# A relational graph layer on one core: messages for unsorted edges, carried in the sorted rows, and added as 16-bit parts

## The chip, the cores and the metric

One core of one Trainium2 chip. The metric is the device time of one execution in microseconds. TensorE is called PE here, VectorE DVE, ScalarE ACT, GpSimd POOL and SyncE SP, as the profile has them.

## What is computed

A stack of four graph layers over 3125 nodes of 32 features and 53125 edges, each behind a layer norm with relu and with a residual. The change touches the first, a relational layer used twice in a row:

```python
def _rel_layer(x, src, dst, etypes, V, a, w_loop, bias, activation=None):
    W = jnp.einsum('rb,bio->rio', a, V)              # 20 relations from 8 bases, 32x32 each
    seg = dst.astype(jnp.int32) * R + etypes.astype(jnp.int32)
    agg = jax.ops.segment_sum(x[src], seg, num_segments=N * R)
    agg = agg.reshape(N, R, -1)
    h = jnp.einsum('nri,rio->no', agg, W) + x @ w_loop + bias
    if activation is not None:
        h = activation(h)
    return h
h = _rel_layer(x, src, dst, etypes, V1, a1, w_loop1, bias1, activation=relu)
h = _rel_layer(h, src, dst, etypes, V2, a2, w_loop2, bias2)
```

That is: each edge carries `x[src] @ W[type]` to its destination node, where the messages are added up. All of it is float32.

## The kernel before

Nodes lie in 25 blocks of 128 (`NB`), one node to a partition. Edges are dealt with in tiles of 128; there are 440 tiles (`T`) once the edges are sorted by the block of their destination and each block is padded to whole tiles. Edges as they come fill 416 columns of 128 (`EC`).

`sort_edges` has two stages. In the first, DVE makes masks of the destination blocks (25 of 128x416), a running count over all of them (one scan of 10400 elements), and, with three small products of PE, the row in the sorted order of every edge (`row`). POOL makes constants and zeroes the records. In the second stage POOL issues one indirect DMA for each of the 416 columns, which scatters the edges' records of 20 words (edge attributes, a one, destination in block, source, type) into `sorted_edges` in DRAM. Beside this, DVE makes the relation weights of both layers from the bases (`relation_weights`, 15 operations each) and the layer norm, PE turns the nodes and makes the message table (`table_stage`: for every node and relation the message of 32 words, 50 products of 320 columns, written to `message_table` in DRAM by SP), and `block_limits` prepares arrays for the last layer.

`add_up_pass` then adds the messages of a layer, in 40 groups of 11 sorted tiles. Of each group 8 tiles have their messages gathered from `message_table` by POOL, an indirect DMA each; for the other 3 they are made on the spot: DVE makes one-hots of the source nodes (25 of 128x384, `sources`), PE picks the nodes' three 16-bit parts with them (`pick`, 25 products), multiplies by the basis parts (`basis_products`) and makes the type's coefficients (`coefficients`), DVE weighs and sums (`weigh`, `messages`). Every tile is added into the accumulator in PSUM by a float32 product of its destination one-hot (made by DVE, `onehots`) with the messages, at a column offset that PE reads from a table (`add`). In the first layer this pass begins with reading the sorted records back, making indices from them (`edge_indices`), and turning source and type rows for the broadcasts of SP (`edge_rows`).

After the first layer the table stage runs again for the second (`after_first`), then `add_up_pass` for it, then three other layers. The order on each engine is the order of the program; the engines wait for one another by semaphores, and the functions in a `with nc.Block()` form a stage, at whose end all engines meet. The steps to follow are `sort_edges` (from line 196, scatters at line 393), `edge_indices` (line 475), `table_stage` (line 624), `add_up_pass` (gathers at 732, source one-hots at 795, terms at 812, sums at 821, picks at 870, adding at 861), `after_first` (line 959).

## Time and profile before

| | |
|---|---|
| time, median of 3 runs | 3484.52 us (3481.57 to 3484.59) |
| profiled execution, its own time | 3477.77 us |
| its span, first to last instruction | 3476.0 us |
| PE busy | 2507.7 us (72%) |
| DVE busy | 2620.6 us (75%) |
| ACT busy | 547.8 us (16%) |
| POOL busy | 2312.8 us (67%) |
| mean granted clock of PE | 0.809 |

A share of busy time is a mean over stages that are bound by different engines, so the profile is read stage by stage: a view by stretches of time first, then the groups of equal instructions, and the timeline where stages meet. POOL's busy time in a transfer is that of making it; the transfer lands later. The granted clock of PE is a share of 2.4 GHz; it takes two levels, 1.2 and 2.4 GHz.

### The profile page before, as it was taken

Reading aid. Unit: us, or ns where it says so; the run is one execution under the profiler, and the core shown is the slowest. Engines: PE = TensorE matmul, PEld = TensorE weight load, DVE = VectorE, ACT = ScalarE, POOL = GpSimd, SP = SyncE. Lnnn points to the kernel's source line nnn. Section 1 sums busy time; section 2 is a strip of 40 time slices with the busy share of each in tenths; the row PEclk is TensorE's granted clock in tenths of the full one; section 3 lists DMA queues with packets and bytes.
Section 4 is the critical chain, followed back from the end, with each engine's and each line's share of the span. In section 5 each row is a group of like instructions: output and inputs, shape, how many; then the busy total and the mean of one; then the engine's idle time right before and its main releaser. Section 6 shows DMA issues by size and latency. Waiting matters only on the chain. (4 is left out here: it accounts for less than half of the span.)

```text
span 3476.0 us, 55173 instructions
## 1 busy us (share of the span) xinstructions
PE 2507.7 (72%) x18522; PEld 1736.9 (50%) x18632; DVE 2620.6 (75%) x7995; ACT 547.8 (16%) x1243; POOL 2312.8 (67%) x2253
## 2 busy tenths in 40 slices
PE   0600000699998999987999699999999867777752
PEld 0300000577875777764666466666666533333331
DVE  9400000799993999979999788888888479999987
ACT  0100000000001000000111122222222123333320
POOL 2777777677770777757777477777777177777740
PEclk9655555688885888878999799999999878888885
DMA  6300000211113111111111100000001011111120
GB/s 100 107 8 8 8 8 8 81 24 26 24 18 100 29 26 25 24 13 34 29 28 28 14 12 11 11 11 11 11 11 11 1 32 27 27 27 27 27 17 5
DMA packets 125181, 91.52 MB, mean 26 GB/s; under 512 B 59702, under 2 KB 110838, under 8 KB 124278
## 3 DMA queue, kind: packets, MB, share of 16 engines
q0 software_dynamic: 70912, 41.10, 8.8%
q1 hardware_dynamic: 54006, 46.92, 5.7%
q8 instruction: 164, 2.69, 0.3%
q14 instruction: 99, 0.81, 0.1%
HBM read 60.45 MB, written 27.41 MB: 25 GB/s over the span
## 5 line engine op out<-in xcount | busy, mean ns | idle before, releaser
L732 POOL DMA_INDIRECT rel_rows<-message_table,message_indices x640 | 645.0, 1008 | 280.1 <-issue 194.5
L1287 POOL DMA_INDIRECT flow_x<-node_table,src_indices x440 | 539.4, 1226 | 227.1 <-issue 104.8
L795 DVE TENSOR_SCALAR rel_source_onehot<-rel_sources,node_numbers 128x384 bf16<-128x384 f16 x2000 | 535.1, 306 | 6.1 <-PE p_rel_picked L870 5.7
L393 POOL DMA_INDIRECT sorted_edges<-stage,sorted_row x416 | 404.3, 972 | 192.0 <-issue 126.5
L1657 POOL DMA_INDIRECT att_kv_rows<-kv_table,att_index x440 | 423.9, 963 | 141.2 <-issue 129.2
L1429 PE MATMUL flow_acc_bwd<-flow_onehot_j,flow_by_q 128*128 128x270 bf16 (+1 forms) x2530 | 493.4, 325 | 7.1 <-issue 0.2
L870 PE MATMUL p_rel_picked<-rel_source_onehot,rel_h_parts 128*96 128x384 bf16 x2000 | 428.5, 383 | 1.0 <-issue 0.7
L870 PEld LDWEIGHTS p_rel_picked<-rel_source_onehot,rel_h_parts 128*96 128x96 bf16 x2000 | 293.6, 148 | 124.6 <-issue 3.8
L1038 POOL DMA_INDIRECT sum_rows<-node_table,src_indices x280 | 270.4, 966 | 110.7 <-issue 85.0
L761 DVE COPY p_rel_lanes<-iota 128x128 f32<-128x128 f32 x2 | 0.6, 295 | 439.4 <-PEq L388 436.7
L664 PE MATMUL p_rel_terms<-ident,source_centred 128*128 128x128 f32 (+1 forms) x4 | 1.1, 435 | 455.2 <-DVE source_centred L650 455.2
L1693 DVE TENSOR_REDUCE att_tile_max<-p_att_scores 128x4 f32<-128x512 f32 x440 | 283.7, 684 | 25.8 <-PE p_att_scores L1807 21.4
L1073 DVE TENSOR_SCALAR sum_source_onehot<-sum_sources,node_numbers 128x512 bf16<-128x512 f16 x1000 | 300.6, 367 | 0.0
L1126 PE MATMUL p_sum_picked<-sum_source_onehot,sum_h_stack 128*96 128x512 bf16 x1000 | 248.8, 411 | 36.8 <-DVE sum_source_onehot L1073 36.3
L1805 PE MATMUL p_att_scores<-att_mask,identb 128*128 128x512 bf16 x440 | 198.2, 450 | 67.0 <-ACT att_parts_turned L1741 67.0
L782 DVE TENSOR_TENSOR rel_onehot<-p_rel_lanes,dst_in_block 128x128 f32<-128x128 f32 x880 | 239.8, 273 | 0.0
L1426 PE MATMUL flow_acc_fwd<-flow_messages,flow_onehot 128*128 128x32 bf16 x1320 | 235.4, 178 | 0.0
L664 PEld LDWEIGHTS p_rel_terms<-ident,source_centred 128*128 128x128 f32 (+1 forms) x4 | 0.7, 202 | 456.5 <-DVE source_centred L650 456.5
L844 ACT CAST rel_picked<-p_rel_picked 96x384 bf16<-96x384 f32 x80 | 38.0, 474 | 1102.1 <-PE p_rel_picked L870 1102.1
L1341 DVE TENSOR_TENSOR flow_by_q<-flow_messages,source_q_mask 128x512 bf16<-128x512 bf16 x330 | 207.2, 681 | 0.0
L1807 PE MATMUL p_att_scores<-att_parts_turned,att_pick 96*128 96x512 bf16 x440 | 201.9, 459 | 0.0
L1426 PEld LDWEIGHTS flow_acc_fwd<-flow_messages,flow_onehot 128*128 128x128 bf16 x1320 | 129.0, 98 | 145.5 <-issue 26.6
(281 smaller groups left out, 4647.5 us busy)
## 6 DMA issues: line engine op xcount, KB each, us to landing
message_table<-message_rows SPq DMA_DIRECT2D x50, 320.0 KB, 2.1
rel_rows<-message_table,message_indices POOLq DMA_INDIRECT x640, 2.5
rel_sources<-source_rows SPq DMA_DIRECT2D x80, 96.0 KB
flow_x<-node_table,src_indices POOLq DMA_INDIRECT x440
att_kv_rows<-kv_table,att_index POOLq DMA_INDIRECT x440, 2.4
sorted_edges<-stage,sorted_row POOLq DMA_INDIRECT x416, 2.1
sum_sources<-source_rows SPq DMA_DIRECT2D x40, 128.0 KB, 3.1
sum_rows<-node_table,src_indices POOLq DMA_INDIRECT x280, 2.4
```

Source lines behind the costliest of these rows:

```text
L393: pool.indirect_dma_start(out=d["sorted"], out_offset=bass.IndirectOffsetOnAxis(ap=row[:, c:c + 1], axis=0), in_=stage[:, c, :], in_offset ...
L732: pool.indirect_dma_start(out=rows[b][:, t, :], out_offset=None, in_=d["messages"], in_offset=bass.IndirectOffsetOnAxis(ap=s["idx_msg"][:, ...
L795: last = dve.tensor_scalar(which[g % 2][:, c, :], srcs[b][:], s["node"][:, c:c + 1], None, ALU.is_equal)
L870: last = pe.matmul(pp[g % 2][0:3 * F, 0:RW], hs[:, c].rearrange("p k f -> p (k f)"), which[g % 2][:, c, :], start=(c == 0), stop=(c == NB ...
L1038: pool.indirect_dma_start(out=rows[b][:, t, :], out_offset=None, in_=d["nodes"], in_offset=bass.IndirectOffsetOnAxis(ap=s["idx_src"][:, g ...
L1073: last = dve.tensor_scalar(which[g % 2][:, c, :], srcs[g % bufs][:], node[:, c:c + 1], None, ALU.is_equal)
L1126: last = pe.matmul(pp[g % 2][0:3 * F, 0:PT * P], hs[:, c].rearrange("p k f -> p (k f)"), which[g % 2][:, c, :], start=(c == 0), stop=(c == ...
L1287: pool.indirect_dma_start(out=X[b][:, t, 0:F], out_offset=None, in_=d["nodes"], in_offset=bass.IndirectOffsetOnAxis(ap=s["idx_src"][:, g * ...
L1426: pe.matmul(accF[:, bass.ds(cols[b, t], F)], hot[b][:, t, :], top(M[b][:])[:, k, t, 0:F], start=False, stop=True, skip_group_check=True)
L1429: last = pe.matmul(accB[:, lo:hi], S[b][:, t, k, :], J[b][:, t, lo:hi], start=False, stop=True, skip_group_check=True)
L1657: pool.indirect_dma_start(out=KV[b][:, t, :], out_offset=None, in_=d["kv"], in_offset=bass.IndirectOffsetOnAxis(ap=ibuf[b][:, t:t + 1], ax ...
L1693: dve.tensor_reduce(tm[b][:, 0, t, :], pR[t % PR][:].rearrange("p (h e) -> p h e", h=HEADS), AX_X, ALU.max).then_inc(max_ready, 1)
```

## The change

Sorting and the making of messages become one stage. The messages of the first layer are made for the edges as they come, in 69 groups of six columns (`CG`): for four (`CP`) by one-hot products as in `add_up_pass`, now 512 wide, for two by gathers from the message table; a tail of two columns is gathered. The messages are put into slots of a ring behind the edge's record, so that a row has 52 words (`ROW`) instead of 20, and POOL scatters each column's rows to their places in the sorted order. DVE has the layer norm ahead of the scan; the relation weights are made by PE from turned bases and coefficients, 32 products a layer; ACT copies the message table out of PSUM and issues its writes; the counts, the limits' turn and the tile map are put between the table products of PE. Rows of padding are written by one DMA from a small tile.

A new stage, `add_sorted`, reads the sorted rows in 20 loads of 22 tiles. ACT and DVE split the messages into three 16-bit parts, DVE makes the destination one-hots of a load in one 16-bit operation, and PE adds with one product of 96 columns for each tile, the three parts side by side; DVE adds the three in the end. The turned rows, the indices for the second layer and the block limits are made at the end of this stage. The second layer's `add_up_pass` is as it was. The semaphores are cleared once more, between the two stages.

The core of the diff (declarations, loads and the unchanged rank steps left out):

```diff
+ROW = REC + F
+CG, CP, SLOTS, RINGS = 6, 4, 6, 4
+AHEAD, BESIDE = 4, 11
...
+                sort_edges(nc, a, s, d, sb, ps, sem, W2)
+                clear_semaphores()
+                relational_layers(nc, a, s, d, sb, ps, sem, W2)
...
+            def _(pool):
...
-                    pool.memset(s["rec"][:], 0.0).then_inc(recs, 1)
...
+                def scatter(g):
+                    b = g % SLOTS
+                    js, c0 = columns(g)
+                    pool.wait_ge(filled, g + 1)
+                    if g < CN:
+                        pool.wait_ge(msg_ready, g + 1)
+                    pool.wait_ge(gathered[b], 16 * (CG - CP) * (g // SLOTS + 1))
+                    for j in js:
+                        c = c0 + j - js[0]
+                        pool.indirect_dma_start(
+                            out=d["sorted"], out_offset=bass.IndirectOffsetOnAxis(ap=row[:, c:c + 1], axis=0),
+                            in_=ring[b][:, j, :], in_offset=None).then_inc(sent[b], 16)
+
+                for g in range(AHEAD):
+                    gather(g)
+                pool.wait_ge(row_ready, 1)
+                pool.wait_ge(pads, 16)
+                for g in range(CN + 1):
+                    if g + AHEAD <= CN:
+                        gather(g + AHEAD)
+                    scatter(g)
...
+            def _(act):
...
+                def fill(g):
+                    slot_free(act, g)
+                    js, c0 = columns(g)
+                    lo, n = js[0], len(js)
+                    act.copy(ring[g % SLOTS][:, lo:lo + n, 0:FE], attr[:, c0:c0 + n, :])
+                    act.copy(ring[g % SLOTS][:, lo:lo + n, FE:REC], meta[:, c0:c0 + n, :]).then_inc(filled, 1)
...
+            def _(dve):
...
+                def sources(g):
+                    b = g % RINGS
+                    dve.wait_ge(row_in[b], 32 * (g // RINGS) + 32)
+                    if g >= 2:
+                        dve.wait_ge(pick_done, g - 1)
+                    for c in range(NB):
+                        last = dve.tensor_scalar(which[g % 2][:, c, :], srcs[b][:], s["node"][:, c:c + 1], None,
+                                                 ALU.is_equal)
+                    last.then_inc(which_ready, 1)
...
+                for g in range(CN):
+                    sources(g)
+                    if g >= 2:
+                        weigh(g - 2)
+                    types(g)
+                    if g >= 2:
+                        messages(g - 2)
...
+            def _(pe):
...
+                def weights(i, banks):
+                    pe.wait_ge(w_in, 64)
+                    v3 = basis[i].rearrange("b (i o) -> b i o", o=F)
+                    for o in range(F):
+                        j, at = divmod(o, F // 2)
+                        last = pe.matmul(banks[j][0:F, at * R:(at + 1) * R], v3[:, :, o], coefT[i][:],
+                                         start=True, stop=True)
+                    last.then_inc(w_made, 1)
...
+                    if n == 2 * BESIDE:
+                        counts()
+                    elif n == 2 * BESIDE + 4:
+                        limits_turned()
+                    elif n == 2 * BESIDE + 6:
+                        tile_map()
...
+                for g in range(CN):
+                    pick(g)
+                    if g >= 1:
+                        basis_products(g - 1)
+                    coefficients(g)
+                basis_products(CN - 1)
...
+LT, LBUFS, HBUFS = 22, 4, 3
+LOADS = T // LT
+PARTED = 3 * F
+def add_sorted(nc, a, s, d, sb, ps, sem, init, finish):
...
+                    for c in range(LOADS):
+                        b = c % LBUFS
+                        act.wait_ge(rows_in[b], 16 * (c // LBUFS) + 16)
+                        if c >= HBUFS:
+                            act.wait_ge(used, c - HBUFS + 1)
+                        act.copy(msg[c % HBUFS][:, :, 0, :], rows[b][:, :, REC:ROW]).then_inc(first_ready, 1)
+                        if c >= 1:
+                            second_part(c - 1)
+                        act.copy(s["dstl"][:, c * LT:(c + 1) * LT], rows[b][:, :, DSTL])
+                        act.copy(s["rec"][:, c * LT:(c + 1) * LT, :], rows[b][:, :, 0:REC]).then_inc(rec_taken, 1)
...
+                        dve.tensor_tensor(hot[c % HBUFS][:], s["iotab"][:].unsqueeze(1).to_broadcast([P, LT, P]),
+                                          dstb[:, mine].unsqueeze(2).to_broadcast([P, LT, P]), ALU.is_equal)\
+                            .then_inc(hot_ready, 1)
+                        if c >= 1:
+                            third_part(c - 1)
+                        dve.wait_ge(first_ready, c + 1)
+                        if c >= 2:
+                            dve.wait_ge(third_ready, c - 1)
+                        dve.tensor_tensor(left[c % 2][:], rows[b][:, :, REC:ROW], msg[c % HBUFS][:, :, 0, :],
+                                          ALU.subtract).then_inc(rest_ready, 1)
...
+                        pe.wait_ge(hot_ready, c + 1)
+                        pe.wait_ge(third_ready, c + 1)
+                        for t in range(LT):
+                            col = pe.snap(regs[t // RG][t % RG], min_val=0, max_val=NB // 5 * BANK - PARTED - F)
+                            last = pe.matmul(acc[:, bass.ds(col, PARTED)], hot[c % HBUFS][:, t, :],
+                                             msg[c % HBUFS][:, t].rearrange("p k f -> p (k f)"),
+                                             start=False, stop=True, skip_group_check=True)
+                        last.then_inc(used, 1)
...
-def relation_weights(a, s, sb, sem, st, layer):
...
-def edge_indices(s, d, sb, sem, st):
```

## Rows read from the trace of the kernel before

In the view by stretches (rows 1) a row has the stretch in us, its length, and for PE, the weight loads PEld, DVE, ACT and POOL the busy time and the count of instructions; then the granted clock, the DMA engines' busy share and GB/s. A timeline row has the start in us, the duration, the engine (an ending q is its queue), the line and operation with the tiles written and read, a count where rows are merged, and the idle time before it with what ended it. A group's row has the line, engine, operation, tiles and shapes, the count, the busy time and the mean in ns, and the idle time ahead.

**Rows 1.** Busy time of each engine by stretch: length, engines, granted clock, DMA.

```profile
77.00:617.00 540.00, 60.98 (x131) 36.23 (x131) 53.66 (x81) 11.70 (x27) 404.35 (x417) 0.53 0.10 24
617.00:652.00 35.00, 13.27 (x60) 12.59 (x61) 22.14 (x69) 0.00 (x0) 22.14 (x25) 0.50 0.52 168
652.00:1061.00 409.00, 397.98 (x2480) 320.17 (x2478) 397.28 (x1522) 26.11 (x80) 301.29 (x298) 0.83 0.16 23
1061.00:1112.00 51.00, 48.91 (x111) 29.55 (x112) 15.61 (x29) 8.93 (x21) 0.00 (x0) 0.53 0.34 129
1600.00:1900.00 300.00, 275.92 (x1833) 180.91 (x1834) 300.00 (x980) 31.65 (x66) 228.01 (x237) 0.93 0.16 29
```

**Rows 2.** Timeline, end of the scatters: start us, us, engine, line.

```profile
607.24 0.96 POOL L393 DMA_INDIRECT sorted_edges<-stage,sorted_row  x1 [0.30 <-issue]
...
616.99 0.16 POOL L721 IOTA node_numbers<- 128x25 f32 x1 [8.78 <-POOLq L388]
...
622.46 0.27 DVE L475 TENSOR_SCALAR index_scratch<-records 128x110 f32<-128x110 f32 x1 [5.16 <-DMA records<-sorted_edges]
```

**Rows 3.** Costliest groups: line, operation, count, busy us, mean ns.

```profile
L732 POOL DMA_INDIRECT rel_rows<-message_table,message_indices x640 | 645.0, 1008 | 280.1 <-issue 194.5
...
L1038 POOL DMA_INDIRECT sum_rows<-node_table,src_indices x280 | 270.4, 966 | 110.7 <-issue 85.0
...
L1341 DVE TENSOR_TENSOR flow_by_q<-flow_messages,source_q_mask 128x512 bf16<-128x512 bf16 x330 | 207.2, 681 | 0.0
```

**Rows 4.** Timeline of the sum layer, one-hots and picks.

```profile
1706.39 3.04 DVE L1073 TENSOR_SCALAR sum_source_onehot<-sum_sources,node_numbers 128x512 bf16<-128x512 f16 x10
...
1708.27 5.57 PE L1126 MATMUL p_sum_picked<-sum_source_onehot,sum_h_stack 128*96 128x512 bf16 x25
...
1716.88 7.28 PE L1126 MATMUL p_sum_picked<-sum_source_onehot,sum_h_stack 128*96 128x512 bf16 x25 [1.00 <-DVE sum_source_onehot L1073]
```

**Rows 5.** Timeline of the second layer's pass, DVE, terms and their sums.

```profile
1235.99 0.94 DVE L812 TENSOR_TENSOR rel_terms<-p_rel_terms,rel_coef 128x768 f32<-128x768 f32 x1
...
1237.18 0.93 DVE L821 TENSOR_REDUCE rel_messages<-rel_terms 128x96 f32<-128x768 f32 x1
```

**Rows 6.** Timeline of the second layer's pass, PE, small products of one group.

```profile
1390.18 0.83 PE L887 MATMUL p_rel_coef<-rel_type_coef,rel_type_onehot 20*128 20x8 f32 x6
...
1391.63 1.19 PE L897 MATMUL p_rel_terms<-rel_basis_parts,rel_picked 96*128 96x256 bf16 x9
```

**Rows 7.** Timeline, a scatter beside DVE's relation weights.

```profile
83.64 1.39 POOL L393 DMA_INDIRECT sorted_edges<-stage,sorted_row  x1 [0.30 <-issue]
...
84.23 0.81 DVE L556 TENSOR_TENSOR w_rel_term<-coef,basis 32x640 f32<-32x640 f32 x1
```

**Rows 8.** Timeline of the opening, POOL and DVE.

```profile
3.30 7.43 POOL L287 MEMSET records<- 128x8800 f32 x1
...
3.41 7.55 DVE L305 TENSOR_SCALAR block_ends<-dst_in 128x416 int32<-128x416 int32 x1 [2.43 <-DMA dst_in<-in_dst]
...
19.44 21.82 DVE L312 TENSOR_TENSOR_SCAN rank<-block_mask 128x10400 f32<-128x10400 f32 x1
...
46.46 14.13 DVE L340 SCALAR_TENSOR_TENSOR rank<-rank,block_offset,block_mask 128x416 f32<-128x416 f32 x25
...
74.43 0.16 DVE L358 TENSOR_TENSOR sorted_row<-sorted_row,extra_row 128x1 uint32<-128x1 uint32 x1
```

**Rows 9.** Timeline, where the first layer's sums are taken.

```profile
1061.32 0.99 DVE L959 TENSOR_SCALAR h_nodes<-rel_acc 128x800 f32<-128x800 f32 x1 [5.47 <-PEq L717]
```

**Rows 10.** Timeline, PE, node turns and the message table.

```profile
100.74 5.71 PE L519 MATMUL p_turn<-ident,h_nodes 128*32 128x128 f32 x25 [52.53 <-DVEq L595]
...
107.10 51.57 PE L624 MATMUL p_message<-w_rel,h_transposed 32*128 32x320 f32 x100 [0.66 <-DVE h_transposed L528]
```

**Rows 11.** Timeline, DVE, first and last step of the block limits.

```profile
171.92 0.38 DVE L430 CAST tile_blocks<-dst_columns 1x440 f32<-1x440 int32 x1
...
180.08 0.18 DVE L439 COPY any_tile_rows<-p_limits 128x25 f32<-128x25 f32 x1
```

813 lines of the change are left out of this document (520 added, 293 removed).

## The prediction

> **What bounds the kernel now.** I read the busy times by stage first, then the costliest groups, then the timeline at the seams of the stages. By stage [rows 1], the first relational layer takes 1061 of the 3476 us of the span, in four pieces: 77 us in which rows of the sorted order are worked out, 540 us of scatters, 35 us of reading back, and 409 us of adding up. In the 540 us POOL is busy for 404 us and everything else for less than 61: the 416 scatters bind alone. In the 409 us PE (398) and DVE (397) are both full and POOL has 301. A POOL transfer costs 1.26 us from start to start: 0.96 us and 0.30 us before the next one [rows 2]. The 320 gathers of this layer's pass are half of the 640 of [rows 3], at 1.008 + 0.30 us. So POOL waits for PE and DVE in one stage, and they wait for POOL in the other. The change puts the two kinds of work side by side. What it costs is a longer start, ahead of that common stage, and a separate stage for adding.
>
> **The common stage, one group.** It has 69 groups of six columns (4 picked by one-hot products, 2 gathered) and a tail of two gathered columns.
> DVE: 25 source one-hots 128x512. Ten in a row took 3.04 us [rows 4], so 25 x 0.30 = 7.5. The terms and the sums are 1024 wide instead of 768: 0.94 and 0.93 us [rows 5] times 4/3, less the 0.07 by which one overlaps the next, 1.15 each. Type one-hot: the two start 1.19 us apart with it between them [rows 5], so 1.19 - 0.87 = 0.32, and 0.4 at 512 columns. Sum 10.2 us.
> POOL: 8 transfers. With the idle DVE's 0.96 it is 8 x 1.26 = 10.1 us; with the 1.008 of the pass with mixed one-hots [rows 3] 8 x 1.31 = 10.5; with the 0.966 beside 512-wide one-hots [rows 3] 10.1. Rows of 208 B instead of 80 B are not shown, but 128 B gathers at 0.966 and 80 B scatters at 0.96 differ by nothing. I take 10.1 to 10.2, nearest to the 512-wide row.
> PE: pick 5.57 us at full clock and 7.28 where the clock fell within it [rows 4]; 12 basis products 4/3 of 1.19 = 1.6; four coefficient products 4/3 of 0.83 = 1.1 [rows 6]. That is 8.3 to 10.0. The sum layer, with the same pick of 25 x 512, was granted 0.93 on average [rows 1].
> ACT fills the slots (two more copies in a group), far below 10 us. SP's two broadcasts per group run three groups ahead.
> All three come out near 10.2, and DVE, POOL and PE hand on to one another; for that I add 0.05: **10.25 us a group**, with ends 10.1 (POOL's cheapest, the one-hots a little closer) and 10.8 (POOL at 1.31, and a little of PE's waits).
>
> **A rule against it.** Beside DVE work a POOL transfer can be longer: with two-input f32 products on DVE a scatter took 1.39 us, not 0.96 [rows 7]. The Trainium skill, SBUF — State Buffer, "SBUF: two separate sides", says that GpSimd cannot write DMA descriptors while DVE holds their shared port pair in a two-port mode; by that, scatters moved under DVE's one-hots would be starved. The trace agrees for the memset and DVE's shift that ran together, 7.43 and 7.55 us [rows 8], and does not for the one-hots: 0.966 us beside them [rows 3]. The terms read PSUM and one SBUF operand, the sums one, so no two-input products stand in the new loop. What a starved POOL would give is the second rival.
>
> **The start, on the path.** Before, DVE's chain ran from the scan (19.4 us) to row numbers at 74.6 us [rows 8]. Now the layer norm lies ahead of the scan: five 128x800 steps of 1 us and small ones [rows 9], 6 us; and the 7.43 us zeroing of the records, beside which DVE's shift waited, is gone; I put the scan at 21 us and its end at 43. Then the counts need PE, which has them in its queue behind the relation weights, the turns and 23 table products. Relation weights: 64 products with 20 columns; the nearest row, the coefficient products, gives 0.25 each [rows 6], the bounds are 0.13 and 0.25, I take 0.2: 13 us. They start when edge columns have been turned, about 12 us: 25 us. The turns take 5.7, the table 51.57 / 50 = 1.03 us a product at half clock [rows 10]: 31 + 23.7 = 55 us. So DVE waits about 12 us for PE (0 if PE keeps its full clock; 16 with the dearer weights). Making the weights on PE frees DVE, which was idle beside the scatters before: worth nothing there, and on the path here. Four more table products, then the limits, 61 us; DVE's 28 us of ranks [rows 8], 89; indices, and the splits of h and of the basis (six steps of 1 us, small ones), 98. The table has been written by about 88 (31 + 52 + the waits for DVE and the landing), so the first 8 gathers (10 us) hide under that. The pad rows, 11.7 MB now, have from 10 to 98 us. Three rounds of one-hots (7.5 each) and the first terms: the first messages are ready at **125 us** (bounds 112 and 135). Before, POOL began at 77: this start costs 48 us.
>
> **The end of it.** 125 + 68 x 10.25 + the last group's six and the tail's two scatters at 1.26 = 832 us. From the last scatter to the next stage 8.8 us passed before [rows 2]; the added clearing of semaphores is bounded by 0 and that, I take 3: **844 us**.
>
> **Adding up sorted rows.** 20 loads of 586 KB; the earlier 1.1 MB reads had the first at DVE after 5.5 us [rows 2], I take 4.5. Per load DVE makes one 128x2816 one-hot from two 16-bit operands, one of them broadcast along its inner axis: the nearest row, a 16-bit product with such an operand, took 0.681 us for 512 [rows 3], about one element a cycle, so 2816 x 1.04 ns + 0.07 = 3.0; at the one-hots' 0.30 for 512 it would be 1.65. Two subtractions of 704 elements at 0.99 for 800 [rows 9] make 1.75 less overlaps, 1.6; the small copy and waits 0.3: **4.9 us, 98 in all** (bounds 70 and 105). PE has 22 products of 96 columns in that time, well below 4.9 us, and ACT four copies of some 2.2 us together. Then 5 reductions of 480 (3 us), last parts and products (4), relu (1), turned edge rows and indices (5; done inside the 35 us stage before), and the block limits, 8.4 us [rows 11], which lay beside scatters before and now have nothing to hide them: 21. Sum 4.5 + 98 + 21 = 124 us, so 968 us. Before, the same point, h ready for the second table, was at 1062 us [rows 9]. **Gain 94 us.** The gathers go from 320 to 140, which is 235 us of POOL; the start takes back 48, the adding 124, less 35 us of reading back, and the adding products leave PE's full pass.
>
> The rest of the kernel issues the same work. The profiled execution took 3477.8 us, 1.8 around its span; the median of the runs is 6.7 above it. 3477.8 - 94 = 3384 for a profiled one; against the median **3390 us**.
>
> **Rivals.** First, PE binds. If the clock stayed at its lower level in the new loop (1.2 GHz), pick and basis products would take twice 5.57 and 1.6, with 1.1 15.4 us a group: + 5.15 x 69 = 355, 3745 us, slower than before. It decides from a chain above 10.25 us, and above 11.6 nothing of the gain is left. For it: 1.1 us of tiny products and 2 us of idleness each group, and 0.53 granted through the second table stage, where PE was busy for 49 of 51 us [rows 1]. Against: 0.93 in the sum layer with the same pick, where 3 us of small products follow it. Chance 0.05.
> Second, POOL is starved: at 1.39 + 0.30 a group is 13.5 us, + 225, 3615 us; it needs 0.17 us more per transfer to eat the gain. Chance 0.06.
> Third, the stages do side by side what they did, and the gain is lost in hand-overs: 11.6 us a group, about 3484, no change that shows. Chance 0.03.
> Fourth, as forecast but with the large one-hot at two elements a cycle (- 27) and PE at full clock in the table (- 12): 3351. Chance 0.10.
>
> **How the numbers follow.** The forecast holds 0.76; its range is 3365 (125 - 13, 10.1) to 3440 (10.8 a group is + 38, start + 10). With the fourth rival, 3345 to 3450. A measurement of this kernel tells about 0.2% (7 us) from no change. Faster: 0.76 + 0.10, and 0.02 of the second rival, where the transfers grow by less than 0.17 us: 0.88; same 0.03; slower 0.05 + 0.04 = 0.09.
>
> **What would show it.** Right: POOL starts its scatters at about 125 us and is busy to about 832 with 0.95 to 1.0 us each; DVE is 98% busy there; the group repeats every 10.1 to 10.5 us; the adding stage's DVE one-hot of 3.0 us repeats every 4.9; the second layer's turns start near 968. Wrong: PE's granted clock near 0.5 in the loop and DVE waiting for the terms; scatters above 1.15 us; a first scatter after 150 us; a wait for the pad rows; or PE, not DVE, setting the 4.9 us.

## Result and the profile after

The changed kernel took 3405.14 us, median of 4 runs (3402.48 to 3406.53), beside 3484.56 us for the kernel before (4 runs on the same chip): a ratio of 0.9772, 95% interval 0.9758 to 0.9786, which is 79 us less (75 to 84). The forecast was 3390 us, a gain of 94. So the direction and the mechanism came out; 15 us of the gain did not. The profiled execution of after took 3402.48 us, its span is 3400.5, and PE's mean granted clock is 0.845 (before 0.809).

Busy time by stretch, the view of [rows 1], for the changed kernel: length, then PE, PE's weight loads, DVE, ACT and POOL, then granted clock, share of the DMA engines, GB/s.

```profile
0.00:117.00 117.00, 71.14 (x269) 43.94 (x269) 74.03 (x109) 32.64 (x75) 12.41 (x28) 0.62 0.76 217
117.00:144.00 27.00, 19.01 (x90) 11.40 (x91) 25.08 (x84) 2.10 (x8) 4.68 (x5) 0.77 0.08 18
144.00:852.00 708.00, 589.04 (x3019) 364.24 (x3018) 678.12 (x1857) 70.44 (x270) 532.86 (x546) 0.89 0.15 33
852.00:866.00 14.00, 12.76 (x57) 11.22 (x56) 11.06 (x9) 5.58 (x11) 0.00 (x0) 0.50 0.70 226
866.00:968.00 102.00, 56.44 (x430) 44.20 (x428) 84.89 (x72) 35.67 (x69) 0.00 (x0) 0.50 0.29 85
968.00:992.00 24.00, 12.04 (x51) 6.64 (x50) 15.56 (x33) 0.00 (x0) 0.00 (x0) 0.55 0.04 9
```

What were two stages, 540 us in which POOL worked alone and 409 us in which PE and DVE were full [rows 1], is one stage of 708 us in which DVE is busy 96% of the time, POOL has 546 transfers, and PE's clock is 0.89. Ahead of it stand 144 us instead of 77, behind it an adding stage in which PE's granted clock is 0.50. No run lays the two kinds of work one behind the other again: that the gain comes from putting them side by side is read from these stretches of before and after. The costliest groups of that stage, from the page (line, operation, count, busy us, mean ns, idle time before them and what ended it):

```profile
L594 DVE TENSOR_SCALAR block_table<-in_sources,node_numbers 128x512 bf16<-128x512 f16 x1725 | 520.0, 371 | 0.8 <-PE p_in_picked L706 0.6
...
L414 POOL DMA_INDIRECT sorted_edges<-block_table,sorted_row x416 | 406.3, 977 | 147.8 <-issue 147.8
...
L400 POOL DMA_INDIRECT block_table<-message_table,message_index_in x140 | 136.5, 975 | 144.6 <-DMA message_table<-message_rows 102.2
```

One group of DVE in the timeline (start us, us, operation); the next group's one-hots start 10.18 us after these:

```profile
508.49 7.59 DVE L594 TENSOR_SCALAR block_table<-in_sources,node_numbers 128x512 bf16<-128x512 f16 x25
516.01 1.20 DVE L609 TENSOR_TENSOR block_table<-p_in_terms,block_table 128x1024 f32<-128x1024 f32 x1
517.14 0.47 DVE L601 TENSOR_SCALAR block_table<-in_types,lane_number 20x512 f32<-20x512 f16 x1
517.54 1.20 DVE L617 TENSOR_REDUCE block_table<-block_table 128x128 f32<-128x1024 f32 x1
518.67 3.50 DVE L594 TENSOR_SCALAR block_table<-in_sources,node_numbers 128x512 bf16<-128x512 f16 x11
```

The start, in the timeline of SP's queue, DVE and POOL, then the lines of ACT and DVE from the view of waits up to 110 us (us in total, times, longest) and two lines of the page's list of DMA issues (KB each, us from issue to landing):

```profile
8.98 0.63 SPq L331 DMA_DIRECT2D sorted_edges<-pad_rows  x1
9.66 42.11 SPq L334 DMA_DIRECT2D records<-in_edge_attr  x1
...
75.34 0.18 DVE L529 TENSOR_SCALAR total_counts<-p_in_picked 128x25 f32<-128x25 f32 x1 [34.05 <-PE p_in_picked L661]
...
117.23 7.61 DVE L594 TENSOR_SCALAR block_table<-in_sources,node_numbers 128x512 bf16<-128x512 f16 x25
...
143.28 6.63 DVE L594 TENSOR_SCALAR block_table<-in_sources,node_numbers 128x512 bf16<-128x512 f16 x25
...
144.14 5.89 POOL L414 DMA_INDIRECT sorted_edges<-block_table,sorted_row  x1 [21.24 <-issue]
150.34 0.97 POOL L414 DMA_INDIRECT sorted_edges<-block_table,sorted_row  x1 [0.30 <-issue]
...
842.20 0.96 POOL L414 DMA_INDIRECT sorted_edges<-block_table,sorted_row  x1 [0.30 <-issue]
```

```profile
ACT message_rows L466 <- DMA message_table<-message_rows: 42.6, 12, 14.7
DVE total_counts L529 <- PE p_in_picked L661: 34.0, 1, 34.0
...
sorted_edges<-pad_rows SPq DMA_DIRECT2D x1, 11440.0 KB, 54.7
...
message_table<-message_rows ACTq DMA_DIRECT2D x25, 320.0 KB, 2.2
```

DVE waits 34 us for the block counts. PE makes them after 23 of the 50 table products, and these stand still because ACT, which empties their banks, waits 42.6 us until the table's blocks have been written. Meanwhile the padding, issued at 8.98 us, is under way for 54.7 us: the table's writes issued up to 55 us land after 6.8 to 16.5 us, most of the later ones after 2.2. (The edge attributes, 3320 KB on the same queue, are read in that time too; no run takes them out, so their share of the waits is open.) From the counts on everything comes in the forecast's spacing.

In the adding stage a load's products, DVE's one-hot with its wait, and DVE's sums at the end:

```profile
908.05 2.94 PE L887 MATMUL rel_acc<-rel_message_parts,rel_onehot 128*128 128x96 bf16 x22 [2.88 <-issue]
913.07 2.87 PE L887 MATMUL rel_acc<-rel_message_parts,rel_onehot 128*128 128x96 bf16 x22 [2.08 <-issue]
...
911.10 3.09 DVE L844 TENSOR_TENSOR rel_onehot<-iota_bf,rel_dst_bf 128x2816 bf16<-128x2816 bf16 x1 [1.04 <-PE rel_acc L887]
...
969.54 2.92 DVE L858 TENSOR_REDUCE h_nodes<-rel_acc 128x160 f32<-128x480 f32 x5 [9.24 <-PE rel_acc L887]
```

PE is idle for 2.1 to 2.9 us ahead of 22 products that take 2.9, waiting for nothing that the profile shows; at this place the program reads the column numbers into registers. DVE, whose own work for a load repeats every 4.83 us where it is not held (863.89 to 868.72 in the timeline), waits for PE.

### The profile page after: what moved, and what is told of

It is laid out like the page before. It is cut to its first block and busy times, and to the rows that moved or that the text cites. A ratio compares the mean times of both kernels' runs of the same rounds, so it can differ in the third digit from the quotient of the medians.

```text
span 3400.5 us, 58425 instructions
## 1 busy us (share of the span) xinstructions
PE 2791.8 (82%) x19728; PEld 1844.5 (54%) x19838; DVE 2957.7 (87%) x8386; ACT 653.1 (19%) x1566; POOL 2125.8 (63%) x2076
## 5 line engine op out<-in xcount | busy, mean ns | idle before, releaser
L706 PE MATMUL p_in_picked<-block_table 128*96 128x512 bf16 x1725 | 446.1, 422 | 106.4 <-DVE block_table L594 106.4
L594 DVE TENSOR_SCALAR block_table<-in_sources,node_numbers 128x512 bf16<-128x512 f16 x1725 | 520.0, 371 | 0.8 <-PE p_in_picked L706 0.6
L1086 POOL DMA_INDIRECT rel_rows<-message_table,message_indices x320 | 322.7, 1008 | 300.2 <-POOLq L1303 203.0
L414 POOL DMA_INDIRECT sorted_edges<-block_table,sorted_row x416 | 406.3, 977 | 147.8 <-issue 147.8
L706 PEld LDWEIGHTS p_in_picked<-block_table 128*96 128x96 bf16 x1725 | 229.5, 136 | 297.2 <-DVE block_table L594 93.6
L1139 DVE TENSOR_SCALAR rel_source_onehot<-rel_sources,node_numbers 128x384 bf16<-128x384 f16 x1000 | 266.6, 306 | 7.0 <-PE p_rel_picked L1212 6.8
L400 POOL DMA_INDIRECT block_table<-message_table,message_index_in x140 | 136.5, 975 | 144.6 <-DMA message_table<-message_rows 102.2
L1212 PE MATMUL p_rel_picked<-rel_source_onehot,rel_h_parts 128*96 128x384 bf16 x1000 | 217.8, 387 | 0.2 <-issue 0.2
L1467 PEld LDWEIGHTS p_sum_picked<-sum_source_onehot,sum_h_stack 128*96 128x96 bf16 x1000 | 130.2, 133 | 141.6 <-DVE sum_source_onehot L1414 37.9
L1770 PEld LDWEIGHTS flow_acc_bwd<-flow_onehot_j,flow_by_q 128*128 128x128 bf16 x2640 | 161.9, 96 | 56.8 <-issue 36.1
## 6 DMA issues: line engine op xcount, KB each, us to landing
sorted_edges<-pad_rows SPq DMA_DIRECT2D x1, 11440.0 KB, 54.7
```

Source lines behind the costliest of these rows:

```text
L414: pool.indirect_dma_start(out=d["sorted"], out_offset=bass.IndirectOffsetOnAxis(ap=row[:, c:c + 1], axis=0), in_=ring[b][:, j, :], in_offs ...
L594: last = dve.tensor_scalar(which[g % 2][:, c, :], srcs[b][:], s["node"][:, c:c + 1], None, ALU.is_equal)
L706: last = pe.matmul(pp[g % 2][0:3 * F, 0:CW], hs[:, c].rearrange("p k f -> p (k f)"), which[g % 2][:, c, :], start=(c == 0), stop=(c == NB ...
L1086: pool.indirect_dma_start(out=rows[b][:, t, :], out_offset=None, in_=d["messages"], in_offset=bass.IndirectOffsetOnAxis(ap=s["idx_msg"][:, ...
L1467: last = pe.matmul(pp[g % 2][0:3 * F, 0:PT * P], hs[:, c].rearrange("p k f -> p (k f)"), which[g % 2][:, c, :], start=(c == 0), stop=(c == ...
L1770: last = pe.matmul(accB[:, lo:hi], S[b][:, t, k, :], J[b][:, t, lo:hi], start=False, stop=True, skip_group_check=True)
```

## Experiments

Theory: the change gains as forecast, by putting POOL's transfers beside DVE's and PE's picks; the missing 15 us lie in the start, where the padding holds the table and the table holds the counts, and in the adding stage, where PE's register loads bind and not DVE. The rivals for each are in the expectations. All ratios are against the kernel before, run beside them; the changed kernel stands at 0.9772, and 0.001 is 3.5 us. From the sums of the adding stage to the end all these kernels issue the same work, and that remainder took 2430 to 2442 us in their profiles, in no relation to the edit. So a whole time tells a stage's gain to some 6 us either way, and the timeline tells it better. "First scatter" is its start, "sums" the start of DVE's sums at the end of the adding stage, both in the profiled run.

| run | ratio to before | first scatter, us | last scatter's end | sums |
|---|---|---|---|---|
| changed kernel | 0.9772 (0.9758 to 0.9786) | 144.1 | 843.2 | 969.5 |
| e1 wide padding | 0.9754 (0.9735 to 0.9774) | 133.4 | 834.1 | 960.6 |
| e2 counts first | 0.9737 (0.9721 to 0.9753) | 126.8 | 825.9 | 952.3 |
| e8 both | 0.9705 (0.9684 to 0.9726) | 114.6 | 814.8 | 941.0 |
| e5 one register load | 0.9745 (0.9728 to 0.9763) | 145.7 | 845.8 | 960.1 |
| e6 third part on POOL | 0.9775 (0.9757 to 0.9793) | 146.4 | 845.7 | 970.1 |
| e7 first scatter free | 0.9789 (0.9770 to 0.9808) | 143.2 | 844.9 | 971.7 |
| e9 start and registers | 0.9664 (0.9642 to 0.9686) | 115.6 | 815.2 | 929.6 |
| e10 four table buffers | 0.9662 (0.9644 to 0.9680) | 110.9 | 810.0 | 924.5 |
| e11 f32 adding | 1.0044 (1.0025 to 1.0062) | 146.9 | 846.0 | 1056.6 |

### The start: padding and counts

```diff
-PADS = 5
+PADS = 20
```

> The padding rows are written in pieces of 4160 B instead of 1040 B (20 rows in a piece instead of 5); nothing else changes. In the changed kernel that write lands 54.7 us after its issue, ACT waits 42.6 us for the message table's own writes meanwhile, and the block counts are done at 74.9 us. Theory (the padding write holds the DMA engines against the table): if its time goes by the piece it lands in 14 to 35 us, the counts are done at 50 to 60 us, the first scatter starts at 122 to 132 instead of 144.1, and the whole takes 3384 to 3393 us. Rival 1 (its time goes by the byte): it still lands after about 50 us or more, counts at about 75, no change in the time (3402 to 3408). Rival 2 (the table is slow for another reason: PE at half clock, two output buffers): it lands sooner, but the counts stay later than 65 us and the time falls by less than 8 us.

The padding took 35.3 us instead of 54.7, so its time goes with the piece as well as with the byte. DVE had the counts at 64.97 us, the first scatter came 10.8 us earlier, the sums 9.0. So the padding does hold the start; but the theory's 50 to 60 us for the counts was missed, since ACT still waited 29.9 us for the table's writes. The whole time fell by 6 us, less than the stage, and its interval overlaps that of the changed kernel. By these numbers rival 2 (the two output buffers) is as near as the theory, and the run with four table buffers, below, shows that it has its part.

```diff
-AHEAD, BESIDE = 4, 11
+AHEAD, BESIDE = 4, 4
...
-                    elif n == 2 * BESIDE + 4:
+                    elif n == 2 * BESIDE + 1:
                         limits_turned()
-                    elif n == 2 * BESIDE + 6:
+                    elif n == 2 * BESIDE + 2:
                         tile_map()
```

> PE makes the block counts after 8 of the 50 table products instead of after 22, and the two small products that follow them one product later each instead of four and six later. Theory (DVE's 34 us wait for the counts is the lost part of the start): the counts are done at 42 to 46 us, row numbers at 76 to 80 instead of 108.8, the first source one-hots at 84 to 88 instead of 117.2. The first pick then waits for PE's table (107), so the first scatter comes at 122 to 128 instead of 144.1, and the whole takes 3383 to 3390 us. Rival (the table's writes hold everything, not the counts): PE, held for DVE inside the table, ends it 5 us or more later, gathers and picks start after 112, and the time falls by less than 10 us.

```profile
43.66 0.19 DVE L529 TENSOR_SCALAR total_counts<-p_in_picked 128x25 f32<-128x25 f32 x1 [1.14 <-PE p_in_picked L661]
...
126.84 5.90 POOL L414 DMA_INDIRECT sorted_edges<-block_table,sorted_row  x1 [5.84 <-issue]
```

DVE's wait of 34.05 us became 1.14, and the first scatter came 17.3 us earlier, as forecast, and not by the whole 34: now DVE's third run of one-hots waits 18.6 us for the first pick, which stands behind the table on PE. The table itself lost nothing (the first gather at 108.7 us instead of 110.3). The 17 us arrive at the sums undiminished.

> The padding in pieces of 4160 B and the counts after 8 table products together. e1 brought the first scatter from 144.1 to 133.4 us (gathers could begin at 99.8 instead of 110.3), e2 to 126.8 (gathers at 108.7, first scatter 18.2 us behind them). Theory (two separate holds on the start: the counts for DVE's chain, the table's writes for PE's first pick): gathers begin at 96 to 101, the first scatter starts at 114 to 120, 24 to 30 us earlier than in the changed kernel, and the stage behind it ends as much earlier: 3374 to 3383 us. Rival (they are one and the same hold): the first scatter stays at 124 to 128 and the time at that of e2, about 3392.

First scatter at 114.6, 29.6 us earlier; the sums 28.5 earlier. That is the sum of e1 and e2 (10.8 + 17.3) within 2 us: two holds, one on DVE's chain and one on the table, and not one and the same.

### The common stage: who binds it

In this run the gathers are left out, and the scatters of the gathered columns read the slots of picked ones:

```diff
                 def gather(g):
-                    b = g % SLOTS
-                    slot_free(pool, g)
...
+                    pass
...
-                            in_=ring[b][:, j, :], in_offset=None).then_inc(sent[b], 16)
+                            in_=ring[b][:, j % CP, :], in_offset=None).then_inc(sent[b], 16)
```

> The 140 gathers are left out; the columns that were gathered are scattered with the messages of picked columns in their place. POOL has 6 transfers a group instead of 8, 7.6 us instead of 10.16; DVE, PE and ACT have the work of before. Theory (DVE binds the common stage, POOL only just fits): the group repeats every 10.0 to 10.2 us, DVE over 97% busy, the time falls by 0 to 15 us. Rival 1 (POOL binds, DVE would be faster if let): the group falls below 9.7 us, the time by more than 35 us. Rival 2 (DVE's one-hots are slowed by POOL's descriptors): 25 one-hots take clearly less than 7.59 us.

```diff
-                    for c in range(NB):
+                    for c in range(19):
                         last = dve.tensor_scalar(which[g % 2][:, c, :], srcs[b][:], ...
...
-                    for c in range(NB):
+                    for c in range(19):
                         last = pe.matmul(pp[g % 2][0:3 * F, 0:CW], ...
```

> DVE makes 19 of the 25 source one-hots of a group and PE the 19 products with them; the source nodes of the last 6 blocks are left out of the messages. DVE has 8.4 us of work a group instead of 10.2, PE about 2 us less; POOL has its 8 transfers. Theory (POOL is at its limit as well): the group stays at 10.1 to 10.2 us, POOL without idle time beyond its 0.30 us between transfers, DVE 82 to 85% busy, and the time falls by 0 to 8 us (3 groups at the start are shorter). Rival (DVE binds alone, POOL has room): the group falls to 8.5 to 9.3 us and the time by 60 to 115 us.

> e3 and e4 together: no gathers, and 19 of 25 one-hots and their products; the columns that were gathered carry the messages of picked columns, and the source nodes of the last 6 blocks are left out. e3 alone gave 6 us, e4 alone none. Theory (DVE and POOL each bind the common stage at 10.0 to 10.2 us a group, so that only both together make it shorter): DVE has 8.5 us a group, POOL 7.6 and now and then 4 us more where a transfer is held by the one-hots, the group falls to 8.4 to 9.2, the time by 70 to 115 us. Rival (something else keeps the group near 10 us, PE's half clock or the hand-overs): it stays above 9.6, the time within 40 us of the changed kernel's.

The busy times in the stage, in the columns of the stretches above, of the changed kernel, e3, e4 and e12:

```profile
200.00:820.00 620.00, 539.07 (x2749) 332.89 (x2750) 615.57 (x1689) 64.15 (x246) 471.53 (x488) 0.90 0.16 34
...
200.00:820.00 620.00, 543.83 (x2756) 334.93 (x2754) 613.95 (x1688) 64.14 (x246) 418.67 (x368) 0.89 0.12 31
...
200.00:820.00 620.00, 459.43 (x2313) 281.74 (x2311) 503.57 (x1289) 57.37 (x239) 474.91 (x477) 0.83 0.14 33
...
200.00:700.00 500.00, 441.51 (x2337) 278.64 (x2335) 496.41 (x1298) 63.10 (x242) 378.63 (x359) 0.91 0.15 37
```

Each of the three was timed once. Without the gathers, a quarter of POOL's transfers, the run took 3396.4 us, 9 less; first scatter to the end of the last one took 693.9 us instead of 699.0, DVE busy 614 of 620 us. With 19 one-hots instead of 25 it took 3414.3, 9 more where 0 to 8 less were expected, and that stretch 712 us, although DVE was idle for a fifth of it: POOL's transfers took 13 us more in sum, 8 of them in two held scatters (below). With both it took 3281.3, and the stretch 579 us: 120 less, with a group every 8.4 us. So DVE and POOL each bind this stage alone, at the same length, and relieving one is worth next to nothing. PE, busy for 544 of 620 us in e3, does not bind. In all runs with the whole work POOL needs 699 to 702 us from first scatter to last, wherever it starts, and this is why a microsecond gained at the start is one gained at the sums. POOL has no gap there beyond 0.30 us from transfer to transfer: 546 x (0.97 + 0.30) is 693, and 5 more are in the first scatter.

That first scatter took 5.89 us instead of 0.96, and e3 and e4 show more like it. From e3's timeline, a scatter that is held, one that is not, and the one-hots beside them:

```profile
171.34 6.63 DVE L584 TENSOR_SCALAR block_table<-in_sources,node_numbers 128x512 bf16<-128x512 f16 x25
...
172.18 5.93 POOL L404 DMA_INDIRECT sorted_edges<-block_table,sorted_row  x1 [2.49 <-DVE block_table L607]
...
505.02 7.82 DVE L584 TENSOR_SCALAR block_table<-in_sources,node_numbers 128x512 bf16<-128x512 f16 x25
...
516.25 1.12 POOL L404 DMA_INDIRECT sorted_edges<-block_table,sorted_row  x1 [2.50 <-DVE block_table L607]
```

From e4's timeline, with a run of 19:

```profile
268.87 5.06 DVE L594 TENSOR_SCALAR block_table<-in_sources,node_numbers 128x512 bf16<-128x512 f16 x19
...
268.96 5.10 POOL L414 DMA_INDIRECT sorted_edges<-block_table,sorted_row  x1 [0.30 <-issue]
```

A held transfer ends 0.13 us after the last one-hot of the run (178.11 and 177.97; 274.06 and 273.93; in the changed kernel 150.03 and 149.91), and a shorter run holds it for less. While it is held, a one-hot takes 0.265 us (6.63 / 25); beside flowing transfers 0.304 (7.59 / 25). With no transfer beside them 25 one-hots took 6.64 us as well (at 125.16 us in the changed kernel). So one of the two goes at its own pace and the other pays, and rival 2 of e3 is true in part: 0.95 of DVE's 10.18 us a group is the price of POOL's transfers beside it. Not each start inside a run is held: in e3 40 scatters started there after a wait, nearly all 0.83 us into the run, and 14 were held; in e12 10 of 27. And two of e4's three held ones came without a wait, like the one shown.

```diff
                             in_=ring[b][:, j, :], in_offset=None).then_inc(sent[b], 16)
+                        if g == 0 and j == 0:
+                            pool.sem_inc(first_out, 1)
...
                 for g in range(CN):
+                    if g == 3:
+                        dve.wait_ge(first_out, 1)
                     sources(g)
```

> DVE begins the one-hots of the fourth group only when POOL has issued its first scatter. In the changed kernel that scatter starts 0.86 us after these one-hots and takes 5.89 us instead of 0.96, ending 0.12 us after the last of them; with 19 one-hots it took 4.32. Theory (DVE's run of one-hots keeps POOL from writing descriptors, and POOL, busy from its first scatter to its last, binds the stage): the first scatter takes 0.95 to 1.2 us, the next ones come beside the one-hots at 0.95 to 1.0, the last scatter ends 3 to 5 us earlier and the whole takes 3398 to 3402 us. Rival 1 (a first scatter is long for reasons of its own): 5.9 us again, DVE loses 6 us more. Rival 2 (DVE binds the stage): the scatter is short, and the stage ends 1 to 2 us later, by DVE's wait.

```profile
143.03 7.90 DVE L596 TENSOR_SCALAR block_table<-in_sources,node_numbers 128x512 bf16<-128x512 f16 x25 [0.61 <-POOLq L418]
...
153.51 6.64 DVE L596 TENSOR_SCALAR block_table<-in_sources,node_numbers 128x512 bf16<-128x512 f16 x25
...
143.21 1.04 POOL L414 DMA_INDIRECT sorted_edges<-block_table,sorted_row  x1 [20.16 <-issue]
154.36 5.91 POOL L414 DMA_INDIRECT sorted_edges<-block_table,sorted_row  x1 [1.07 <-issue]
```

The first scatter took 1.04 us, though it too began inside the run, 0.18 us after its start: a first scatter is not long for reasons of its own, and rival 1 falls. But the gain did not come. POOL, now ahead of DVE, ran out of work 11 us later, and the first scatter of the second group met the next run and was held for 5.91 us; the last scatter ended 1.8 us later than in the changed kernel, which is what rival 2 (DVE binds) gave. After that hold POOL is behind DVE for the rest of the stage and no further scatter is held. Where POOL does not wait the hold is rare: none of the first transfers in 66 runs of one-hots of the changed kernel, two in e4. Where it has just waited it came in 24 of 67 cases (e3 and e12). What decides is open.

### The adding stage

```diff
-                    regs = [[pe.alloc_register(f"rel1_col{i}{t}") for t in range(RG)] for i in range(2)]
+                    regs = [pe.alloc_register(f"rel1_col{t}") for t in range(LT)]
...
-                        for j in range(LT // RG):
-                            load_aligned(pe, unused, regs[j], s["dcol"][0:1, 2, :], c * LT + j * RG)
+                        load_aligned(pe, unused, regs, s["dcol"][0:1, 2, :], c * LT)
```

> In the adding stage PE reads the 22 column numbers of a load with one load into 22 registers instead of two into 11. In the changed kernel PE is idle 2.05 to 2.9 us ahead of each load's 22 products (2.9 us), and DVE, whose own work repeats every 4.83 us where nothing holds it, waits up to 1.0 us for PE. Theory (these register loads, at a cost per load, set the 5.2 to 5.8 us of a load): PE's idle time falls to 1.0 to 1.5 us, a load repeats every 4.8 to 4.9 us, the last product ends 8 to 13 us earlier, the whole takes 3391 to 3397 us. Rival (the cost goes by the register, or PE is slowed by its half clock alone): the idle time stays above 1.9 us, the time within 3 us of 3405.

```profile
904.79 3.12 PE L886 MATMUL rel_acc<-rel_message_parts,rel_onehot 128*128 128x96 bf16 x22 [1.88 <-DVE rel_message_parts L833]
909.55 3.01 PE L886 MATMUL rel_acc<-rel_message_parts,rel_onehot 128*128 128x96 bf16 x22 [1.64 <-DVE rel_message_parts L833]
...
904.87 3.09 DVE L844 TENSOR_TENSOR rel_onehot<-iota_bf,rel_dst_bf 128x2816 bf16<-128x2816 bf16 x1
909.70 3.09 DVE L844 TENSOR_TENSOR rel_onehot<-iota_bf,rel_dst_bf 128x2816 bf16<-128x2816 bf16 x1
```

A load repeats every 4.83 us, DVE no longer waits, and PE now waits for DVE's third part. From DVE's first load to the last sum's start the stage takes 102.9 us instead of 114.7: 11.8 less. The theory holds. What one load of 22 registers costs is not seen, since PE's 1.64 to 1.88 us of idleness ends with DVE.

```diff
-                        if c >= 1:
-                            third_part(c - 1)
...
+                @block.gpsimd
+                def _(pool):
+                    for c in range(LOADS):
+                        pool.wait_ge(second_ready, c + 1)
+                        pool.tensor_tensor(msg[c % HBUFS][:, :, 2, :], left[c % 2][:], msg[c % HBUFS][:, :, 1, :],
+                                           ALU.subtract).then_inc(third_ready, 1)
```

> As e5_one_register_load, and the third part of the messages (0.88 us on DVE for each load) is made by POOL, which has nothing else to do in that stage. Theory (DVE binds the adding stage once the register loads are cheaper): DVE repeats every 3.95 us, PE with 2.9 and 1.0 to 1.5 us sets 4.0 to 4.4, the last product ends 8 to 17 us earlier than in e5, the whole takes 3376 to 3388 us. Rival (POOL's subtraction takes over 3 us or slows DVE's work beside it): a load repeats every 4.8 us or more, no gain over e5 or a loss.

```profile
907.27 2.20 DVE L852 TENSOR_TENSOR rel_message_rest<-rel_rows,rel_message_parts 128x704 f32<-128x704 f32 x1
...
905.02 3.71 POOL L833 TENSOR_TENSOR rel_message_parts<-rel_message_rest,rel_message_parts 128x704 bf16<-128x704 f32 x1 [1.63 <-ACT rel_message_parts L815]
```

The rival came true, in both its parts: POOL's subtraction takes 3.71 us where DVE's took 0.88, and DVE's own subtraction beside it takes 2.20 instead of 0.88. DVE gave 0.88 us away and got 1.32 back; a load repeats every 5.34 us.

The part of the change that adds in 16-bit parts, undone (with two buffers for the one-hots instead of three):

```diff
-            hot = [sb(st1, f"rel1_onehot{b}", [P, LT, P], BF16) for b in range(HBUFS)]
+            hot = [sb(st1, f"rel1_onehot{b}", [P, LT, P]) for b in range(HBUFS)]
...
-                            last = pe.matmul(acc[:, bass.ds(col, PARTED)], hot[c % HBUFS][:, t, :],
-                                             msg[c % HBUFS][:, t].rearrange("p k f -> p (k f)"),
+                            last = pe.matmul(acc[:, bass.ds(col, F)], hot[c % HBUFS][:, t, :],
+                                             rows[c % LBUFS][:, t, REC:ROW],
```

> One part of the change undone: the sorted rows are added as float32, by products of 32 columns of a float32 one-hot, and not as three 16-bit parts of 96 columns. DVE keeps the one-hot (2816 elements, about 3.1 us) and drops the copy and two subtractions of 1.9; ACT drops two casts. PE: such a float32 product took 0.117 us at the higher clock in the kernel before, 0.234 at the lower. Theory (float32 products at half clock bind): 22 products take 5.2 us, with 2.1 us of register loads 7.3 a load, the last product ends 35 to 50 us later than in the changed kernel, the whole takes 3435 to 3455 us. Rival (PE is at its higher clock there, or its weights load beside it): 4.7 to 5.2 us a load, no loss or a gain of up to 12 us: 3393 to 3405.

From the groups of the adding stage in the 190 us of that run from 870 on, and, as the last line, eight such products in the timeline of the kernel before:

```profile
L858 PE MATMUL rel_acc<-rel_rows,rel_onehot 128*128 128x32 f32 x875 | 186.9, 401 | 0.0
L858 PEld LDWEIGHTS rel_acc<-rel_rows,rel_onehot 128*128 128x128 f32 x875 | 186.8, 333 | 0.0
L824 DVE TENSOR_TENSOR rel_onehot<-iota,rel_rows 128x2816 f32<-128x2816 f32 x18 | 55.7, 3092 | 121.2 <-PE rel_acc L858 121.2
...
706.62 1.87 PE L861 MATMUL rel_acc<-rel_rows,rel_onehot 128*128 128x32 f32 x16
```

PE is busy without a gap, at a granted clock of 0.50, and its weight loads as long as its products; DVE's one-hots of two loads start 9.38 us apart (906.53 and 915.91), so a product costs 9.38 / 22 = 0.43 us with its weights. That is nearly twice the 0.23 expected, because the 0.117 behind it is a record of the trace and not a product: a float32 product has two records (880 for the 440 tiles), and eight of them took 1.87 us before, 0.234 each, at a granted clock of 1.00. The 2.1 us of register loads, on the other hand, do not show: the run has the same two for each load, and PE has no idle time, so they pass while products are at work. The run lost 95 us against the changed kernel, 1.0044 of the time before: without the 16-bit parts the whole change gains nothing. They are the part that makes a separate adding stage affordable.

### Together

> The three edits that gained, together: padding in pieces of 4160 B, counts after 8 table products, one register load for 22 columns. e8 had its first scatter at 114.6 us and 3379 us, e5 took 11.9 us off the adding stage. Theory (the start and the adding stage lie one behind the other with POOL's 699 us between them, so that the gains add): first scatter at 113 to 117, adding loop 102 to 104 us from DVE's first load to the last product, the whole 3366 to 3372 us. Rival (a later stage gives part of it back): above 3375.

The sums came 39.9 us earlier than in the changed kernel (e8's 28.5 and the 11.8 of e5's adding stage make 40.3), and the whole took 3369.51 us, 0.9664 of before: as expected. The gains add because POOL's 699 us stand between them.

```diff
-        y = [sb(st, f"message_rows1{i}", [P, R * F]) for i in range(2)]
+        y = [sb(st, f"message_rows1{i}", [P, R * F]) for i in range(4)]
```

> As e9_start_and_registers, with four buffers for the message table's blocks between ACT and their write instead of two. In e8 ACT still waited 32.3 us in 11 waits for these writes, the table ended at 94.7 us, and PE's first pick began at 95.8, while DVE had its first one-hots ready from 88.7. Theory (the padding still holds the table by its buffers): the waits fall under 12 us, the table ends at 78 to 88 us, the first scatter comes at 103 to 109, bounded by DVE's third run of one-hots (96.2 + 7.6) and a group's terms and sums, the whole takes 3355 to 3364 us. Rival (the DMA engines are full, more buffers only queue more): the waits move to the end, the table ends after 91, no gain over e9.

ACT's waits for the table's writes fell from 32.3 us in e8 to 2.7, so more buffers do let the table pass beside the padding. But PE then reaches its place for the counts before DVE has counted, and waits 8.0 us there: its last table product ends at 89.9 us (94.9 in e9), not at 78 to 88. The first scatter came at 110.9, not 103 to 109, and the sums 5.1 us earlier than in e9. The whole time is e9's within its interval. It is the fastest kernel here, 3367.47 us, and faster than the changed kernel by some 38 us.

## Why the prediction came out as it did

| point, us | forecast | profile of after |
|---|---|---|
| scan starts | 21 | 18.9 |
| DVE has the counts | 55 | 75.3 |
| first source one-hots | 98 | 117.2 |
| first messages ready | 125 | 143.4 |
| last scatter ends | 832 | 843.2 |
| next stage | 844 | 851.1 |
| second layer's turns | 968 | 986.7 |

The group: right, and in the right place. 10.25 us were forecast and 10.18 came, with DVE's terms as worked out (7.59, 1.20, 0.47 and 1.20 against 7.5, 1.15, 0.4 and 1.15, less overlaps) and POOL at 0.96 to 0.99 a transfer. That all three come out near 10.2 held for DVE and POOL to a degree which the text did not draw out: e3, e4 and e12 show that either alone keeps the group there. PE has room: its pick takes 5.6 us in 37 of the groups and 7.0 to 8.6 in the others, at a granted clock of 0.89 over the stage. The rival in which PE binds at half clock did not come.

The start: wrong by 18 us, and in one step. The spacing was right, from the scan to the counts aside: the counts to the one-hots 41.9 us (43 forecast), the one-hots to the messages 26.1 (27). Wrong was that the table's products would run at 1.03 us each up to the counts, and with it the sentence that the padding has from 10 to 98 us. Four products that nothing held took 4.63 us, so the rate was near; the holds between them were left out. The row behind 1.03 [rows 10] is from a table made with no large write beside it. The padding was priced as a load that must be done in time, and not as one that fills the engines that ACT's writes of the table also need. e1 shortened the padding and e2 took the counts out of its reach; each brought back its part. The two buffers of the table count as well: with four, ACT's waits fell to 2.7 us. The Trainium skill, DMA: Bandwidth & Descriptors, "Queues, rings and completion order", says that SP's and ACT's queues each have one ring on each of the same 16 DMA engines, which take packets from them in turn. The trace agrees in so far as writes on ACT's queue landed after 6.8 to 16.5 us beside those on SP's, and after 2.2 later. The relation weights by PE were priced at 13 us and took 7.6 (3.81 and 3.79), by themselves a gain of 5 that the wait for the counts swallowed.

The end of the stage: 843.2 - 143.4 is 700 us, and 707 were forecast. The groups were cheaper, but the last two come 2.9 us apart, without one-hots to make, so that POOL ends with 15 transfers still to start and not with 8. The clearing of semaphores, bounded by 0 and put at 3, costs nothing that shows: 7.9 us from the last scatter's end to the next stage's first DMA.

The adding stage: DVE's work was right, 3.09 us for the one-hot (3.0 forecast) and 4.83 for a load (4.9). The step that failed is "PE has 22 products of 96 columns in that time, well below 4.9 us". The products take 2.9 us, at a granted clock of 0.50, and ahead of them PE is idle for 2.1 to 2.9 more, at the place of the two register loads, which the text doesn't count. That is what the list of signs called PE, not DVE, setting the 4.9 us. e5, with one register load instead of two, took 11.8 us off. The loads bind only because the products are short: under e11's 9.4 us of products for each load they cost nothing. PE also began late, after 10.87 us of float32 products for the layer's own weights. The tail was put at 21 us and took 17.1.

The starved POOL: a chance of 0.06 was given to it, and the row against it (0.966 us beside one-hots [rows 3]) was read too broadly. It holds for most transfers that follow one another. A scatter that started while a run of one-hots was under way was held to its end once here, 14 times in e3, 10 in e12 and 3 in e4. A hold of 5 us in each group would have cost more than the rival's 13.5 us a group; here POOL is full and does not wait, and one hold was paid for in 699 us. The Trainium skill, SBUF — State Buffer, "SBUF: two separate sides", calls the pair of ports an exclusive lock that whichever starts first has "for the whole instruction". The trace agrees in part: held scatters ended 0.12 to 0.13 us after DVE's last one-hot. But the hold lasted 5.9 us, over some 22 instructions of 0.265 us, and not one; most scatters that started inside a run (43 of 67 in e3 and e12) were not held; and that the held ones wait for these ports is not shown.

The sum, in lateness against the forecast: first messages 18.4 us late; the last scatter's end 11.2 (the common stage gave 7.2 back); the next stage's first DMA 7.1 (the clearing, 4.1); the sums of the adding stage 23.0, of which its loop is 16.7 (114.7 for 98) and a quicker first load takes 0.7 back; the second layer's turns 18.7 (the tail took 3.9 less; the rest is rounding). From there the rest took 2413.9 us (3400.5 - 986.65), and before it took 2413.7 from the same point (3476.0 less the end of [rows 9], 1062.31): nothing behind was touched, as forecast. Between the two profiled executions the gain is therefore 75.3 us where 94 were forecast. The medians are 4 us further apart, since that of before lies 6.8 us above its profile and that of after 2.7. That the whole came within 0.5% of the forecast is luck in part: 18.4 us at the start and 16.7 in the adding loop stand against 7.2, 4.1 and 3.9 given back elsewhere.

## What to carry to other kernels

Two engines that are each full at the same length must be relieved together; a stage of that kind passes on every microsecond by which it starts earlier, so the start is where to look first. Price a large background transfer by who else needs the DMA engines while it runs, and put small products on which a long chain waits ahead of the bulk in PE's queue. Count what an engine does between its instructions, register loads above all, against the period of the loop, where its own work is too short to hide it.

## What the runs showed of the hardware

- An indirect DMA of POOL that starts in a run of 16-bit one-hots on DVE can be held to the end of the run (5.8 to 5.9 us with 25 of them, 4.2 to 5.1 with 19), and the one-hots then took 0.265 us instead of 0.304. After a wait of POOL 24 of 67 such starts were held, without one two in e4; of scatters that started 0.83 us into the run some took 5.93 us and some 1.12. What decides is open.
- A float32 subtraction of 128x704 on POOL took 3.71 us, and one of DVE beside it 2.20 instead of 0.88.
- 11440 KB of padding took 54.7 us in pieces of 1040 B and 35.3 in pieces of 4160 B, with the same transfers issued beside it.
- With two loads of 11 registers ahead of each 22 products PE showed 2.1 to 2.9 us of idle time where the products took 2.9 us, and none where they took 9.4.
- A float32 product of 128x128 weights with 32 columns took 0.43 us at a granted clock of 0.50 (0.234 at 1.00, in the kernel before); the three 16-bit parts, 96 columns, 0.13 at 0.50 (2.9 / 22).
